# A block kernel's prologue: extra throwaway products in TensorE's pauses, and step 0's state and output put ahead of step 1's transposed blocks

## The chip, the core and the metric

One core of a Trainium2 chip runs the whole program. The metric is device microseconds of one execution; what is compared is the median of several executions.

## The reference, cut to what matters

```python
x = L0_attn_out                                   # (4, 2048, 256)
mod = (silu(c) @ wmod) -> sa, ca, ga, sb, cb, gb  # six rows of 256 for each batch
h = layernorm(x) * (1 + ca) + sa
# attention: rk = h / |h| per head, wk = rk one token earlier, v = h @ Ww.T; chunks of 64 tokens
A = inv(I + tril(wk wk^T * decay, -1))            # per chunk and head, 64 x 64
for chunk in 32 chunks:                           # S: 64 x 64 for each head
    v_new = A @ v - (A @ wk) @ S
    o = (rk * decay) @ S + intra @ v_new
    S = decay**64 * S + (wk * tail).T @ v_new
x = x + ga * (h + (alpha * o) @ Wr.T)
h = layernorm(x) * (1 + cb) + sb
u = silu(h @ w1 * s1) * (h @ w2 * s2)             # 256 -> 1024
u = gelu(u @ h1 * sh1); u = gelu(u @ h2 * sh2)    # 1024 -> 1024, ternary weights
x = x + gb * (u @ w3 * s3)                        # 1024 -> 256
```

## The kernel before, in words

The 2048 tokens are 32 steps of 64. One step takes 64 tokens of all four batches: 256 columns for the dense layers. Each step has an attention part, which hands a state on to the next step, and a dense part (`l1`, `l2`, `l3`, `y`), in which each 128x128 block of ternary weights is multiplied by a rounded high part and a low part of the activations. The attention of a step runs beside the dense part of an earlier one.

Each engine has its own program, and every engine's program is generated from one written list of items: `alone`, then `opening`, then `second`, `third` and `mixed` (steady state, in a hardware loop). An engine skips items that are not its own, and takes its own in the order of the list. So if an item moves in a list, it moves in the queue of every engine that has a part of it. Each engine's queue is in order: an instruction that waits for a semaphore holds everything behind it.

Before the dense layers can start (the first product of `l1`, line 1249) the prologue has to be done. It has these pieces, named as in the lists:

- The modulation rows: `shift(0)` and `shift(1)` (line 1561), and, when the second part of `wmod` has landed, 32 small products with 4 columns (line 1578). VectorE makes columns and gates of them (lines 1150 to 1168), and behind that `unit` of step 0, the normalised rows `r` (line 929).
- `start` turns `h` and `r` on TensorE (lines 1384 and 1388); `gram` multiplies the turned rows with themselves (line 1419); ScalarE copies the result (line 797); GpSimd masks it (line 648).
- `fs`, `expand`, `n` invert the triangular blocks. `n` 3 ends with ScalarE's copy to `diag` (line 751). `solve` 0 is `own` (line 1222) and `inner` (line 1215), `solve` 1 is `corner` (line 1232), and ScalarE copies the new values `vn` (line 756).
- `state` (lines 1534 and 1536, then two copies on VectorE, lines 1059 and 1060), `attn_out` (line 1545, then lines 1070 to 897 on VectorE, and a power on GpSimd, line 636), `norm2` (line 1079), `turn` (line 1554), `ln2` (ScalarE, line 832), `parts` (VectorE, lines 1085 and 1087), and then `l1`.
- For step 1, as far as it is ready: `stats`, `norm`, `square`, `length`, `unit`, `start`, `gram`, `intra`, `fs`, `values`, `pred`. `square` overwrites `r`, so it waits until the last token's row has been copied out by SP (`last_in`, line 531). For step 1 there is a power on GpSimd in `length`.
- `check` on ScalarE (line 766) runs through 11 parts of the raw weights as they land and sums their low bits. `check` 2 is parts 2, 3 and 4; `check` 3 and 4 are one part each; `check` 5 is the last four parts. After the last one `flag` tells whether any bit was set: VectorE reduces, TensorE turns the column, VectorE reduces again, and TensorE reads the flag (`value_load`) and takes one of two programs, the exact one only if a weight isn't representable.
- `warm` (line 1238) multiplies a tile of ones into a bank that nobody reads. `round` casts weights (GpSimd line 659, ScalarE line 771). `residual` is two products on GpSimd (lines 678, 680).

An fp32 product shows as two matmul records in the trace.

Of the kernel before, what the change touches and what calls it, by code (L numbers as in the profile page):

```python
# [15 lines left out]
P = 128  # L16
# [45 lines left out]


CHECKS = {0: (0,), 1: (1,), 2: (2, 3, 4), 3: (5,), 4: (6,), 5: (7, 8, 9, 10)}
WARM_START, WARM_CHAIN, WARM_LINK, WARM_FLAG, WARM_JUMP = 3, 4, 1, 2, 1
ROUNDS_ACT = {2: (4, 5)} | {3 + k: (6 + k,) for k in range(11)}
ROUNDS_POOL = {0: (0, 2), 1: (1, 3)} | {5 + k: (17 + k,) for k in range(5)}

# [44 lines left out]
def main(nc, ctx, sb, sem, sems, x, wts, wv, wr, wmod, cT, scales, s3, decay, const, out):  # L113
# [5 lines left out]
    duo = [ctx.enter_context(nc.psum_tensor(f"duo{i}", [P, 2, 512], F32)) for i in range(2)]  # L119
# [23 lines left out]
    state = sb("state", [NP, 2, DH])  # L143
# [141 lines left out]
    def listed(first, columns, between):  # L285
# [26 lines left out]
    alone = [(*item, 0) if len(item) == 2 else item for item in (  # L312
        ("check", 0), ("ready", 0), ("start", 0), ("spread", 0), ("tables", 0), ("gram", 0), ("heads", 0), ("check", 1), ("values", 0), ("gates", 0), ("warm", WARM_CHAIN),
        ("intra", 0), ("fs", 0), ("fs", 1), ("fs", 2), ("fs", 3), ("expand", 0), ("far", 0), ("stats", 0, 1), ("check", 2), ("n", 1),
        ("warm", WARM_LINK), ("n", 2), ("warm", WARM_LINK), ("n", 3), ("heads", 1), ("warm", WARM_LINK), ("norm", 0, 1), ("round", 0), ("square", 0, 1), ("length", 0, 1),
        ("solve", 0), ("check", 3), ("unit", 0, 1), ("wr", 0), ("keys", 0), ("solve", 1), ("start", 0, 1), ("check", 4), ("round", 1), ("residual", 0), ("state", 0),
        ("gram", 1, 1), ("rg", 0, 1), ("intra", 0, 1), ("check", 5), ("fs", 0, 1), ("attn_out", 0), ("values", 0, 1), ("pred", 0, 1), ("warm_end", WARM_FLAG))]

    opening = [(*item, 0) for item in (
        ("norm2", 0), ("turn", 0), ("fs", 1), ("flag", 0), ("u", 0), ("flag", 1), ("ln2", 0), ("ln2", 1), ("parts", 0), ("residual", 0),
        ("round", 2), ("silu", 0))]
    second = listed([], layers[:2 * HK], {
        ("l1", 0): [("fs", 2, 0)],
        ("l1", 2): [("fs", 3, 0)],
# [58 lines left out]
    def begun(n, items):  # L385

        if items is mixed:
            return min(n + 2, STEPS) if isinstance(n, int) else n + 2
        return 3 if items is third else n + 1
# [87 lines left out]
    with nc.Block() as block:  # L477
# [156 lines left out]
        def _(pool):  # L634
# [17 lines left out]
            def step(n, g, items):  # L652
                def part(name, k, a, phase):
                    now, p = a + 1, phase % 2
                    if name == "round":
                        for u in ROUNDS_POOL.get(k, ()):
                            slot = slice(SLOT * u, SLOT * (u + 1))
                            pool.wait_ge(checked, u // UNIT_SLOTS + 1)
                            pool.tensor_copy(w_hi[:, slot, :], w_raw[:, slot, :]).then_inc(rounded[1], 1)
                    if name == "ready":  # L660
                        pool.wait_ge(near_tables, 1)
                    if name == "stats":
                        stats(a)
                    if name == "length":
                        length(a)
                    if name == "residual":

                        if items is alone:
                            pool.wait_ge(gates_ready, NB)
                        if items is alone:  # L670
                            pool.wait_ge(r_ready, 2)
                        if items is opening:
                            pool.wait_ge(xl_ready, n)
                        pool.wait_ge(h_ready, now)
                        after(pool, x1_ready, a - 2)
                        if items is mixed or items is third and a == n + 2:
                            pool.wait_ge(r_turned, a - 3)
                        pool.tensor_tensor(base[phase % BASES][:], h_of(a)[:], ga, ALU.mult).then_inc(gah_ready, 1)
                        pool.wait_ge(gah_ready, now)
                        pool.tensor_tensor(base[phase % BASES][:], x_of(a)[:], base[phase % BASES][:], ALU.add).then_inc(base_ready, 1)  # L680
                    if name == "rg":
                        if items is alone:
                            pool.wait_ge(heads_ready, 1)
                        pool.wait_ge(rT_ready, now)
                        pool.tensor_tensor(rg[:].rearrange("p (b q) c n -> p b (q c) n", b=NB),
                                           rT[p][:].rearrange("p (b q) c n -> p b (q c) n", b=NB)[:, :, :, 1:C + 1],
                                           head_decay[:].rearrange("p q c n -> p (q c) n").unsqueeze(1).to_broadcast([P, NB, H, C]),
                                           ALU.mult).then_inc(rg_ready, 1)
                    if name == "gram":
                        for e in range(2):  # L690
                            pool.wait_ge(gram_ready[e], now)
                            ins = masked(near, 0, e)
                        ins.then_inc(near_ready, 1)
                        for e in range(2):
                            ins = masked(cross, 1, e)
                        ins.then_inc(cross_ready, 1)
                    if name == "l1":
                        pool.wait_ge(l1_hi, nth(n, k))
                        pool.tensor_tensor(act_lo[0][:, k, :], full[k % 3][:], act_hi[0][:, k, :].bitcast(F32), ALU.subtract).then_inc(l_ready[0], 1)  # L699
                    if name == "far":  # L700

                        if items is alone:
                            pool.wait_ge(inv_ready, now)
                        after(pool, mi_full, a)
                        for e in range(2):
                            ins = masked(far, 2, e)
                        ins.then_inc(far_ready, 1)
                    if (name == "lead" or name == "solve" and k == 0) and items is not alone:
                        pool.wait_ge(inter_full, a)
                        by_head = state[:].rearrange("p (b q) c d -> p b q (c d)", b=NB)  # L710
                        pool.tensor_tensor(by_head, by_head, chunk_decay[:].unsqueeze(1).unsqueeze(3).to_broadcast([P, NB, H // 2, 2 * DH]),
                                           ALU.mult).then_inc(state_decayed, 1)
                    if name == "attn_out":
                        pool.wait_ge(ln2_ve, now)
                        rsqrt(rstd2, ve2, ln2_rstd)

                walk(part, n, g, items)
# [475 lines left out]
        def _(pe):  # L1193
# [40 lines left out]

            def warm(count, bank, cols=512):

                for _ in range(count * 512 // cols):
                    pe.matmul(bank[:, 0:cols], o_state[:, 0, :], o_state[:].rearrange("p q n -> p (q n)")[:, 0:cols], start=True, stop=True)

            def step(general, n, g, items):  # L1240
# [88 lines left out]
                def part(name, k, a, phase):  # L1329
# [25 lines left out]
                                mm = pe.transpose(mlp[b][:, i * P:(i + 1) * P], gate_cols[:, i // KT, i % KT, 2 * b:2 * b + 2, :].rearrange("p b n -> p (b n)"), ident)  # L1355
                            mm.then_inc(gates_spread, 1)
                    if name == "warm":
                        warm(k, duo[0][:, 1, :], P)
                    if name == "warm_end":
                        warm(k, duo[1][:, 1, :])  # L1360
                    if name == "flag" and k == 0:
                        pe.wait_ge(flag_col, 1)
                        pe.transpose(duo[1][0:1, 1, 0:P], any_low[:], ident).then_inc(flag_row, 1)
                        warm(WARM_JUMP, duo[1][:, 0, :])
                    if name == "ready":
                        pe.wait_ge(small_in, 5 * 16)
                    if name == "tables":
# [7 lines left out]
                    if name == "start":  # L1375
# [6 lines left out]
                        for kt in range(KT):  # L1382
                            for b in range(NB):
                                mm = pe.transpose(in_h[:, (b * KT + kt) * P:(b * KT + kt + 1) * P], h_a[:, b, kt * P:(kt + 1) * P], ident)
                        mm.then_inc(hT_full, 1)
                        pe.wait_ge(r_ready, now)
                        for q, (b, hp) in enumerate(pair_of):
                            mm = pe.transpose(in_r[:, q * P:(q + 1) * P], r[:, b, hp * P:(hp + 1) * P], ident)
# [32 lines left out]
                    if name == "pred":  # L1421
# [2 lines left out]
                            pe.wait_ge(ao_scaled, n)  # L1424
                            pe.wait_ge(state_ready, n)
                        if items is not mixed:
                            pe.wait_ge(hT_ready, now if items is alone else begun(n, items))
                            pe.wait_ge(rT_ready, now if items is alone else begun(n, items))
                        if items is alone:
                            pe.wait_ge(state_ready, a)  # L1430
                        for q, c, e in blocks:
                            mm = pe.matmul(duo[0][half(c), e, q * DH:(q + 1) * DH], rT[p][half(e), q, c, 0:C],  # L1432
# [130 lines left out]
                mm.then_inc(mod_full, 1)  # L1563

            pe.wait_ge(warm_set, 1)
            warm(WARM_START, mlp[1][:], P)
            pe.wait_ge(spread_done, 1)
            pe.wait_ge(wmod_in[0], 16)
            shift(0)
            pe.wait_ge(pow_ready, 1)  # L1570
            pe.transpose(solo[1][0:H, 0:P], powers[:], ident).then_inc(pow_turned, 1)
            shift(1)

            pe.wait_ge(spread_done, 2)
            pe.wait_ge(wmod_in[1], 16)
# [3 lines left out]
            mm.then_inc(col_full, 1)  # L1579
            first_step(lambda *args: step(False, *args))  # L1580
            pe.wait_ge(flag_set, 1)
            warm(WARM_JUMP, duo[1][:, 1, :])
            any_bits = pe.value_load(flag_i[0:1, 0:1], min_val=0, max_val=1)
            with pe.If(any_bits < 1):
                program(False)
# [43 lines left out]
```

## Time and profile before

| | us |
|---|---|
| median of 3 runs | 1703.91 |
| lowest, highest | 1701.28, 1704.21 |
| the profiled execution, its own time | 1700.03 |
| its span in the trace | 1698.1 |

| engine | busy us | share of the span |
|---|---|---|
| TensorE (PE) | 1677.2 | 99% |
| VectorE (DVE) | 1144.6 | 67% |
| ScalarE (ACT) | 1004.8 | 59% |
| GpSimd (POOL) | 596.6 | 35% |

Starts are microseconds from the start of the span. The granted clock (PEclk) is TensorE's, as a share of 2.4 GHz; it has two levels, 0.50 (1.2 GHz) and 1.00 (2.4 GHz), and a value between them is a stretch with both. "issue" as the releaser of a wait is time in which nothing that the profile shows was waited for.

### The profile page before, as it was taken

How to read it: one execution, taken by the hardware profiler on the slowest of the kernel's cores; microseconds unless marked ns; L12 is line 12 of the kernel's file. 1: busy time of each engine (PE TensorE's matmuls, PEld its weight loads, DVE VectorE, ACT ScalarE, POOL GpSimd, SP SyncE). 2: the span in 40 equal slices, each digit the busy share in tenths (PEclk: the TensorE clock that was granted, in tenths of full speed). 3: DMA queues.
4: the chain of work that ended last, by engine and by line, in shares of the span. 5: the costliest groups of instructions: out<-in, count | busy, mean ns of one | idle time of the engine just before them, and what ended most of it. 6: DMA issues, size and time to landing. Idle time of an engine off the chain costs nothing.

```text
span 1698.1 us, 59356 instructions
## 1 busy us (share of the span) xinstructions
PE 1677.2 (99%) x24310; PEld 1619.7 (95%) x24310; DVE 1144.6 (67%) x3223; ACT 1004.8 (59%) x2389; POOL 596.6 (35%) x694
## 2 busy tenths in 40 slices
PE   8899999999999999999999999999999999999998
PEld 7798999999999999999999999999999999999998
DVE  5777667776666776766776766776766776766432
ACT  4764665556656556666556665555665555665554
POOL 3544333343333243433243333234333234333101
PEclk8899999999999999999999999999999999999999
DMA  8202223332223332222332222322222332222110
GB/s 279 89 21 41 49 47 61 55 55 43 50 48 56 55 58 42 49 48 56 56 57 44 49 49 53 61 52 44 51 50 49 61 54 44 52 49 42 21 20 8
DMA packets 396492, 92.13 MB, mean 54 GB/s; under 512 B 368372, under 2 KB 388472, under 8 KB 396216
## 3 DMA queue, kind: packets, MB, share of 16 engines
q1 hardware_dynamic: 394224, 85.87, 25.8%
q8 instruction: 197, 3.23, 0.8%
q10 hardware_dynamic: 1992, 2.38, 0.5%
q14 instruction: 79, 0.65, 0.1%
HBM read 45.07 MB, written 30.94 MB: 45 GB/s over the span
## 4 chain that ended last, share of the span: by engine, by line
PE 94%; DVE 2%; POOL 1%; DMA 1%; issue 1%; ACT 1%; SPq 0%; ACTq 0%; DVEq 0%; POOLq 0%
PE mlp L1249 66%; PE mlp L1323 7%; PE solo L1249 3%; PE solo L1407 3%; PE duo L1545 3%; PE solo L1222 2%; PE duo L1215 1%; PE solo L1232 1%; PE duo L1432 1%; PE duo L1210 1%; PE duo L1534 1%; PE duo L1419 1%; PE duo L1536 1%; PE duo L1455 1%; POOL act_lo L699 1%
## 5 line engine op out<-in xcount | busy, mean ns | idle before, releaser
L1249 PE MATMUL mlp<-act_hi,w_hi 128*128 128x256 f32 x4096 | 975.1, 283 | 1.2 <-POOL act_lo L699 0.6
L1249 PE MATMUL mlp<-act_lo,w_hi 128*128 128x256 f32 x4096 | 954.5, 278 | 0.0
L1249 PEld LDWEIGHTS mlp<-act_hi,w_hi 128*128 128x128 f32 x4096 | 771.2, 188 | 12.0 <-POOL act_lo L699 1.4
L1249 PEld LDWEIGHTS mlp<-act_lo,w_hi 128*128 128x128 f32 x4096 | 771.8, 188 | 0.8
L858 ACT ACTIVATE full<-mlp,scale_sb 128x256 f32<-128x256 f32 x512 | 242.6, 474 | 444.1 <-PE mlp L1249 441.8
L961 DVE TENSOR_TENSOR act_lo<-full,act_hi 128x256 fp32r<-128x256 f32 x512 | 260.3, 508 | 276.4 <-ACT act_hi L859 274.2
L699 POOL TENSOR_TENSOR act_lo<-full,act_hi 128x256 fp32r<-128x256 f32 x256 | 186.9, 736 | 484.5 <-ACT act_hi L848 484.5
L859 ACT ACTIVATE act_hi<-mlp,scale_sb 128x256 fp32r<-128x256 f32 x512 | 240.1, 469 | 0.0
L1249 PE MATMUL mlp<-xh,w_hi 128*128 128x256 f32 x768 | 180.5, 278 | 1.3 <-DVE full L1093 1.3
L1249 PE MATMUL mlp<-xl,w_hi 128*128 128x256 f32 x768 | 179.7, 277 | 0.0
L1093 DVE SCALAR_TENSOR_TENSOR full<-mlp,scale_sb,gate 128x256 f32<-128x256 f32 x192 | 92.7, 484 | 87.4 <-ACT gate L843 83.3
L1249 PEld LDWEIGHTS mlp<-xh,w_hi 128*128 128x128 f32 x768 | 144.3, 188 | 3.2 <-DVE full L1093 1.7
L843 ACT ACTIVATE gate<-mlp,scale_sb 128x256 f32<-128x256 f32 x192 | 91.4, 476 | 91.7 <-PE mlp L1249 76.0
L1249 PEld LDWEIGHTS mlp<-xl,w_hi 128*128 128x128 f32 x768 | 144.3, 188 | 0.0
L636 POOL TENSOR_TENSOR rinv<-ssm,minus_half 128x8 f32<-128x8 f32 x32 | 52.8, 1650 | 204.0 <-DVE ssm L926 204.0
L1323 PE MATMUL mlp<-w_hi,act_hi 128*128 128x256 f32 x512 | 122.4, 281 | 0.0
L1323 PE MATMUL mlp<-w_hi,act_lo 128*128 128x256 f32 x512 | 121.8, 279 | 0.0
L848 ACT CAST act_hi<-full 128x256 fp32r<-128x256 f32 x256 | 101.8, 398 | 12.8 <-DVE full L1093 12.8
L648 POOL TENSOR_TENSOR near<-gram,level_mask 128x256 f32<-128x256 f32 x64 | 45.9, 738 | 152.8 <-ACT gram L797 152.8
L1323 PEld LDWEIGHTS mlp<-w_hi,act_hi 128*128 128x128 f32 x512 | 96.1, 188 | 0.1
L1323 PEld LDWEIGHTS mlp<-w_hi,act_lo 128*128 128x128 f32 x512 | 96.1, 188 | 0.0
L636 POOL TENSOR_TENSOR rstd<-ve,minus_half 128x2 f32<-128x2 f32 x64 | 48.2, 754 | 124.4 <-DVE ve L897 121.7
(198 smaller groups left out, 2734.7 us busy)
## 6 DMA issues: line engine op xcount, KB each, us to landing
w_raw<-in_wts SPq DMA_DIRECT2D x22, 512.0 KB, 5.2
kg<-r SPq DMA_DIRECT2D x64, 126.0 KB
xin<-in_x SPq DMA_DIRECT2D x62, 128.0 KB, 2.8
out_y<-y SPq DMA_DIRECT2D x62, 128.0 KB, 2.5
x_squares<-o_state SPq DMA_DIRECT2D x30, 256.0 KB, 3.2
vn<-x_squares SPq DMA_DIRECT2D x120, 64.0 KB, 2.2
h_squares<-near SPq DMA_DIRECT2D x28, 256.0 KB, 3.3
hT<-h_squares SPq DMA_DIRECT2D x112, 64.0 KB, 2.2
```

The lines of the kernel that those rows point to most:

```text
L636: pool.tensor_tensor(dst[:], src[:], minus_half[:, 0:src.shape[1]], ALU.pow).then_inc(done, 1)
L699: pool.tensor_tensor(act_lo[0][:, k, :], full[k % 3][:], act_hi[0][:, k, :].bitcast(F32), ALU.subtract).then_inc(l_ready[0], 1)
L843: act.activation(gate[k % 2][:], gated[k % 3][:, 0:TOK], ACT.Silu, scale=scale_sb[:, 0, k:k + 1]).then_inc(l_act[0], 1)
L848: act.copy(act_hi[0][:, j, :], full[j % 3][:]).then_inc(l1_hi, 1)
L858: act.activation(full[k % 2][:], mlp[k % 2][:, 0:TOK], ACT.Gelu, scale=s)
L859: act.activation(act_hi[layer % 2][:, k, :], mlp[k % 2][:, 0:TOK], ACT.Gelu, scale=s).then_inc(l_act[layer], 1)
L961: dve.tensor_tensor(act_lo[layer % 2][:, k, :], full[k % 2][:], act_hi[layer % 2][:, k, :].bitcast(F32), ALU.subtract).then_inc(l_ready[la ...
L1093: dve.scalar_tensor_tensor(full[k % 3][:], up, s, gate[k % 2][:], ALU.mult, ALU.mult).then_inc(prod_ready, 1)
L1249: mm = pe.matmul(dst, *general_ops, start=is_first and i == 0, stop=is_last and i == 1)
L1323: mm = pe.matmul(mlp[k][:, 0:D], *ops, start=j == 0 and i == 0, stop=j == HK - 1 and i == 1)
L1407: mm = pe.matmul(solo[0][:, b * D:(b + 1) * D], hT[:, b, kt, :], wv_sb[:, kt, :], start=kt == 0, stop=kt == KT - 1)
L1545: mm = pe.matmul(duo[1][:, 0, b * D:(b + 1) * D], o_state[:, b * (H // 2) + hp, :], wr_turned[:, hp, :], start=hp == 0, stop=hp == H // 2 - 1)
```

## The change

Only the prologue's lists and throwaway products change; the lists `second`, `third` and `mixed` are as they were.

1. Throwaway products. `WARM_START` and the three `WARM_LINK` and `WARM_CHAIN` products have 512 columns each and no longer 128 (four times fewer products for as many columns); `WARM_CHAIN` is 5 and no longer 4. New: 2 products of 512 behind `shift(1)`, 3 between the two halves of step 0's `start`, 2 ahead of step 1's `gram`. Near the flag, products are cut to 128 columns: 12 of them (1536 columns, before 1024) in `warm_end`, 8 (1024 columns, before 512) in `flag`, 4 (512 columns, as before) ahead of the `value_load`.
2. `residual` 0, `keys` 0 and `wr` 0 come ahead of step 1's `square`. On GpSimd `residual` 0 now waits for the second `h` instead of the second `r`. `round` 1 comes ahead of `solve`.
3. `state` 0 comes ahead of step 1's `unit`, and `attn_out` 0 ahead of step 1's `start`.
4. `values`, `pred`, `intra` and `fs` 0 of step 1, and `warm_end`, go from `alone` to `opening`, behind `norm2` and `turn`.

```diff
-WARM_START, WARM_CHAIN, WARM_LINK, WARM_FLAG, WARM_JUMP = 3, 4, 1, 2, 1
+WARM_START, WARM_SHIFT, WARM_TURN, WARM_CHAIN, WARM_LINK, WARM_GRAM, WARM_FLAG, WARM_JUMP = 3, 2, 3, 5, 1, 2, 3, 1
+PIECE_FLAG, PIECE_JUMP = 128, 128
...
-        ("warm", WARM_LINK), ("n", 2), ("warm", WARM_LINK), ("n", 3), ("heads", 1), ("warm", WARM_LINK), ("norm", 0, 1), ("round", 0), ("square", 0, 1), ("length", 0, 1),
-        ("solve", 0), ("check", 3), ("unit", 0, 1), ("wr", 0), ("keys", 0), ("solve", 1), ("start", 0, 1), ("check", 4), ("round", 1), ("residual", 0), ("state", 0),
-        ("gram", 1, 1), ("rg", 0, 1), ("intra", 0, 1), ("check", 5), ("fs", 0, 1), ("attn_out", 0), ("values", 0, 1), ("pred", 0, 1), ("warm_end", WARM_FLAG))]
+        ("warm", WARM_LINK), ("n", 2), ("warm", WARM_LINK), ("n", 3), ("heads", 1), ("warm", WARM_LINK), ("norm", 0, 1), ("round", 0), ("residual", 0),
+        ("keys", 0), ("wr", 0), ("square", 0, 1), ("length", 0, 1), ("round", 1), ("solve", 0), ("solve", 1), ("check", 3), ("state", 0), ("unit", 0, 1),
+        ("attn_out", 0), ("start", 0, 1), ("check", 4), ("warm_wait", WARM_GRAM), ("gram", 1, 1), ("rg", 0, 1), ("check", 5))]
...
-        ("norm2", 0), ("turn", 0), ("fs", 1), ("flag", 0), ("u", 0), ("flag", 1), ("ln2", 0), ("ln2", 1), ("parts", 0), ("residual", 0),
-        ("round", 2), ("silu", 0))]
+        ("norm2", 0), ("turn", 0), ("values", 0), ("pred", 0), ("warm_end", WARM_FLAG), ("intra", 0), ("fs", 0), ("fs", 1), ("flag", 0), ("u", 0), ("flag", 1), ("ln2", 0), ("ln2", 1),
+        ("parts", 0), ("residual", 0), ("round", 2), ("silu", 0))]
...
                         if items is alone:
-                            pool.wait_ge(r_ready, 2)
+                            pool.wait_ge(h_ready, 2)
...
-                for _ in range(count * 512 // cols):
+                for _ in range(count * (512 // cols)):
...
                     if name == "warm":
-                        warm(k, duo[0][:, 1, :], P)
+                        warm(k, duo[0][:, 1, :])
+                    if name == "warm_wait":
+                        warm(k, solo[1][:])
                     if name == "warm_end":
-                        warm(k, duo[1][:, 1, :])
+                        warm(k, duo[1][:, 1, :], PIECE_FLAG)
...
                         pe.transpose(duo[1][0:1, 1, 0:P], any_low[:], ident).then_inc(flag_row, 1)
-                        warm(WARM_JUMP, duo[1][:, 0, :])
+                        warm(2 * WARM_JUMP, duo[1][:, 0, :], PIECE_JUMP)
...
                         mm.then_inc(hT_full, 1)
+                        if items is alone and a == 0:
+                            warm(WARM_TURN, mlp[1][:])
                         pe.wait_ge(r_ready, now)
...
-                            pe.wait_ge(hT_ready, now if items is alone else begun(n, items))
-                            pe.wait_ge(rT_ready, now if items is alone else begun(n, items))
-                        if items is alone:
+                            pe.wait_ge(hT_ready, begun(n, items))
+                            pe.wait_ge(rT_ready, begun(n, items))
+                        if items is opening:
                             pe.wait_ge(state_ready, a)
...
-            warm(WARM_START, mlp[1][:], P)
+            warm(WARM_START, mlp[1][:])
...
             shift(1)
+            warm(WARM_SHIFT, mlp[1][:])
...
-            warm(WARM_JUMP, duo[1][:, 1, :])
+            warm(WARM_JUMP, duo[1][:, 1, :], PIECE_JUMP)
```

## Rows read from the trace of the kernel before

**Rows 1.** Windows: stretch, its length, busy us (instructions) per engine, granted clock, DMA share, GB/s

```profile
12.60:18.80 6.20, 6.20 (x30) 5.83 (x29) 3.87 (x16) 1.86 (x2) 1.94 (x2) 0.50 0.62 202
26.20:39.80 13.60, 11.95 (x232) 10.85 (x232) 10.37 (x50) 8.31 (x11) 4.50 (x6) 1.00 0.94 332
39.80:50.10 10.30, 8.97 (x164) 8.32 (x163) 7.80 (x9) 5.93 (x8) 7.14 (x5) 0.51 0.93 316
60.30:63.80 3.50, 3.46 (x5) 1.11 (x5) 2.09 (x5) 3.50 (x10) 0.00 (x0) 0.52 0.03 7
200.00:1000.00 800.00, 799.96 (x11827) 778.12 (x11826) 561.38 (x1586) 477.19 (x1163) 282.00 (x324) 1.00 0.28 52
```

**Rows 2.** Timeline of TensorE's products: start, us, line, tiles, shape, records, idle before

```profile
11.73 6.15 PE L1578 MATMUL mlp<-scT,wmod_sb 128*128 128x4 f32 x32 [1.80 <-DMA wmod_sb<-in_wmod]
...
27.85 3.74 PE L1238 MATMUL duo<-o_state 128*128 128x128 f32 x32
31.64 1.12 PE L1199 MATMUL duo<-inv,cross 64*64 64x32 f32 x32
...
44.29 1.92 PE L1232 MATMUL solo<-vn,mi 32*32 32x64 f32 x32 [0.52 <-issue]
...
48.36 1.13 PE L1534 MATMUL duo<-intra,vn 64*64 64x64 f32 x32 [0.25 <-issue]
49.24 1.08 PE L1536 MATMUL duo<-vn,kg 64*64 64x64 f32 x32
50.23 0.70 PE L1419 MATMUL mlp<-rT 64*64 64x65 f32 x32
...
60.49 3.54 PE L1238 MATMUL duo<-o_state 128*128 128x512 f32 x4
64.00 0.35 PE L1249 MATMUL mlp<-xh,w_hi 128*128 128x256 f32 x1
```

**Rows 3.** Chain that ended last, 36 to 52: start, us, what

```profile
38.46 1.90 issue
```

**Rows 4.** Timeline of VectorE, lines of square, unit, wr, keys, attn_out and parts

```profile
40.47 0.69 DVE L922 TENSOR_TENSOR r<-x 128x512 f32<-128x512 f32 x1 [1.55 <-DMA last<-r]
...
43.84 1.50 DVE L929 TENSOR_TENSOR r<-x,rinv 128x512 f32<-128x512 f32 x1 [1.75 <-POOL rinv L636]
45.26 2.40 DVE L978 TENSOR_SCALAR wr_turned<-wr_turned,gam 128x256 f32<-128x256 f32 x2
47.58 0.68 DVE L998 TENSOR_TENSOR kg<-kg,tail_decay 128x512 f32<-128x512 f32 x1
...
54.20 0.68 DVE L1070 TENSOR_TENSOR x<-duo,mods 128x512 f32<-128x512 f32 x1
...
57.09 0.17 DVE L897 TENSOR_SCALAR ve<-mv 128x2 f32<-128x2 f32 x1
...
63.16 0.69 DVE L1087 TENSOR_TENSOR xl<-h,xh 128x512 fp32r<-128x512 f32 x1
```

**Rows 5.** Timeline of ScalarE, parts 4 and last of check, diag, vn, gram

```profile
33.07 1.91 ACT L766 ACTIVATE low_bits<-w_raw 128x2048 f32<-128x2048 uint16 x1 [0.33 <-DMA w_raw<-in_wts]
...
37.08 0.84 ACT L751 ACTIVATE diag<-duo,con 128x256 f32<-128x256 f32 x2 [2.00 <-PE duo L1466]
...
46.24 0.59 ACT L756 COPY vn<-solo 128x512 f32<-128x512 f32 x1 [0.16 <-PE solo L1232]
...
50.98 0.65 ACT L797 COPY gram<-mlp 128x256 f32<-128x256 f32 x2 [1.21 <-PE mlp L1419]
...
57.81 1.91 ACT L766 ACTIVATE low_bits<-w_raw 128x2048 f32<-128x2048 uint16 x1
```

**Rows 6.** DMA queues, 38 to 39: packets, MB, share of 16 engines' time

```profile
q8 instruction: 1, 0.02, 6.0%
```

**Rows 7.** Timeline of GpSimd, step 1's power in length

```profile
42.17 1.64 POOL L636 TENSOR_TENSOR rinv<-ssm,minus_half 128x8 f32<-128x8 f32 x1 [6.26 <-DVE ssm L926]
```

**Rows 8.** Timeline of weight loads, the first one of l1 behind the flag

```profile
63.97 0.19 PEld L1249 LDWEIGHTS mlp<-xh,w_hi 128*128 128x128 f32 x1 [1.43 <-issue]
```

## The prediction

> **What bounds the kernel now.** I read the page first: TensorE is busy for 99% of the span. Then the windows: from 200 to 1000 us it is busy for 799.96 of 800 us at granted clock 1.00 [rows 1]. No list of that stretch is edited, so it stays as long as it is. What can move is the moment at which the dense layers start, the first product of l1 at 64.00 [rows 2]; whatever it moves by, the end moves by: what follows is built on it in every engine, and in the long stretch TensorE has no idle time that could take a shift up. So the case is a prologue of 64.0 us, of which the edits can reach some part.
>
> In the prologue the windows show the clock at 0.50 in three stretches: 12.60 to 18.80, 39.80 to 50.10, and 60.30 to 63.80 [rows 1]. TensorE had paused before each: 1.80 us for wmod [rows 2], 1.90 us in own [rows 3], and before the flag. At 0.50 a run of 32 small products takes 1.92 us and at 1.00 it takes 1.12; a record with 128 columns takes 3.74 / 32 = 0.117 us at 1.00 and 3.54 / 16 = 0.221 at 0.50 (the four 512-column records count as 16) [rows 2].
>
> Then I asked what l1 waits for, going backwards through the timelines. It starts at 64.00; xl is written at 63.16 + 0.69 = 63.85 [rows 4]; ahead of that stand ln2 and the last check on ScalarE, which starts at 57.81, and ScalarE goes from its copy of gram at 50.98 through the four checks of check 5 without a pause [rows 5]. Call the start of that copy G. Last check = G + 6.83, xl = G + 12.87, l1 = G + 13.02. The edited lists keep check 5 whole and behind gram, and ln2 behind it. So **two numbers decide: G, and how long after G l1 starts**, where the products behind the flag now count: they begin at 60.49 = G + 9.51 and end when l1 starts [rows 2].
>
> **The change part by part: what comes before G.**
>
> (a) The two products behind shift(1) (512 columns, two records each: 16 x 0.117 = 1.9 us) fill the 1.80 us pause [rows 2] and cost nothing. If the clock stays, the 32 records of line 1578 take about half of their 6.15 us and end near 14.8 and not at 17.88. Behind it gates, unit, start, gram and fs are earlier, by at most 3.1 us and at the least by none (the 3 products in start add 24 x 0.117 = 2.8 us at full clock, 5.3 at half, and lie in the wait for r). From about 1.3 upwards it no longer matters which: ScalarE can't copy to diag before part 4 of check is done. That check waited for its DMA, starts at 33.07, and with 1.91 and some 0.2 for reading its sum (an estimate by the smallest row, 0.17 [rows 4]) ends near 35.2 [rows 5]; the loads are not edited, and the DMA share is 0.94 [rows 1]. So diag starts at 35.2 instead of 37.08: -1.9. I take this end, since the expected lead is 1.3 to 2.6. The other end is 38.4 (+1.3, rival 3).
>
> (b) From diag to vn: before from 37.08 + 0.84 = 37.92 to 46.24 + 0.59 = 46.83 [rows 5], 8.9 us. In it is a pause of 1.90 us in the middle of own, in which nothing awaited is seen, and after which the clock is 0.51 [rows 1, 3]. New at full clock: own 1.12, inner 1.12, a copy 0.35 (half of the gram copy's 0.65), corner 1.12, vn 0.59, and five hand-overs of 0.05: 4.55, to 36.0 + 4.55 = 40.6. With the pause 42.5. With everything at half clock and the pause: 3 x 1.92 + 0.35 + 0.59 + 0.25 + 1.9 = 8.85, to 44.9.
> Which? The queue that brings instructions has one packet just as TensorE stands still [rows 6]; the pause looks like a missing block of instructions. The edits take some 50 records and their weight loads out of the queue ahead, so that the block's end falls into inner and no longer into own; behind it the consumption is as fast and the DMA engines are as loaded. I keep the pause, and take 42.5.
> The Trainium skill, "Runtime: NRT & Kernel Launch", section Instruction fetch mechanics, says that crossing a block boundary is mostly hidden, since fetching runs ahead of dispatch. The 1.90 us above say otherwise for this stretch. By the rule vn would be there at 40.6, the no-pause end (rival 1).
>
> (c) The VectorE queue before state. In the 1.55 us wait for the DMA of the last row [rows 4] now stand keys (0.68) and wr (2.40, slow beside GpSimd; it will have residual beside it again). norm ends at 40.47 - 1.55 = 38.92 before and 1.9 earlier now, 37.0; 37.0 + 0.68 + 2.40 = 40.1, still ahead of 40.47. So square stays at 40.47, which the DMA sets (it is issued behind loads that don't move), and 3.1 us of later VectorE work are gone. With (a) at nothing, square is late by 1.5. GpSimd's residual moves to the same place and its power is free by 42.0; round 1 sits behind the power and slows unit, as before.
> The Trainium skill, "GPSIMD Engine Reference", section Specifications, says that GpSimd shares VectorE's path to SBUF and contends with instructions that have two SBUF inputs or run in a two-port mode. It speaks against putting keys and wr beside residual; the trace agrees for wr (2.40 for two) and for unit (1.50), not for keys, 0.68 beside residual.
>
> (d) state to G. square, its sum and its floor end at 40.47 + 0.69 + 0.69 + 0.17 = 42.0 [rows 4], the power at 42.1 + 1.64 = 43.75 [rows 7]. state's products took 48.36 to 50.32 at half clock; at full 1.96 x 1.12 / 1.92 = 1.2 [rows 2]: 42.5 + 1.2 = 43.7. VectorE's two copies of 0.69: 45.1. unit 0.68 to 1.50, I take 1.1: 46.2. attn_out, whose products run beside unit, 54.20 to 57.26 = 3.06 on VectorE [rows 4]: 49.2. The rT copies 0.9 (0.69 and 0.17, one gap): 50.1. gram 0.70 [rows 2]: 50.8. **G = 50.9 against 50.98: nothing.** What it costs: step 1's gram, which ScalarE needs before the last four checks, now stands behind attn_out on VectorE; what it gains is that xn is there at 50 instead of 59, but nobody can use it, as ln2 stands behind the checks. The bounds: without the pause VectorE is the limit: 42.0 + 1.38, unit from 43.75 to 44.85, + 3.06 + 0.9 + 0.7 gives G = 49.6 (-1.4). With the pause and the clock fallen behind it (corner 1.92, state 1.96, gram 1.2): 52.9 (+1.9).
>
> **What comes after G.** values and pred are TensorE's before 54, and warm_end (24 records, 2.8 us) ends near 56, though the flag comes at G + 9.2 = 60.1: over 3 us of pause, so I expect half clock at the flag, as before. There are now 16 + 8 = 24 records of 128 columns for 16 before: at half clock as long as the 3.3 us that it took to rise [rows 1], 15 records, then 9 x 0.117 = 1.05: 4.4 us, l1 = G + 13.9. Bounds: at full clock 2.8 us, and xl (G + 12.9) is later; all at half 5.3 us, and up to 1.43 us for reading the flag and the jump, seen as a gap before the first load of l1 [rows 8] but hidden there under the last long product; short pieces hide less: G + 16.2. I take G + 13.9.
>
> **Sum.** l1 at 50.9 + 13.9 = 64.8, +0.8 us. The profiled execution would take 1700.03 + 0.8 = 1700.8; it stands 3.9 below the median of the runs shown, 1703.91, so the median becomes **1704.7**.
>
> **Rivals.**
> Rival 1, the pause goes and the clock holds: G = 49.6, and l1 at xl, G + 12.9 = 62.5: -1.5, 1702.4. For it: three filled pauses; against it: the pause in own was not a wait for data. If the last row's DMA lands 2 us earlier as well (its wait was 1.55 [rows 4]), it is -3.5, 1700.4.
> Rival 2, slower: the pause stays and the clock falls behind it as it did before, since state, attn_out and gram now all stand in one line on it. G = 52.9, l1 = G + 14.9 (one more us for the jump): 67.8, +3.8, 1707.7. It decides if TensorE stands still for 1.9 us in inner. For it: the same pause was followed by 0.51 before. Against it: more columns stand just ahead.
> Rival 3, the clock falls during line 1578 after all, whose products have 4 columns. Then the 3 products in start hold the turn of r: 5.3 us and not 2.8. r is turned 1.3 late, diag 38.4 less what the earlier rise gives back; with the tail of the forecast +2.2, 1706.1.
>
> **How the numbers follow.** What a measurement of this kernel can tell from no change is about 0.2%, 3.4 us: under 1700.5 or over 1707.3. Forecast (a shift within 1 us of +0.8) 0.45, rival 1 0.27 (0.12 of it with the early DMA or luck of the runs, below 1700.5), rival 2 0.18, rival 3 0.10. Same: 0.45 + 0.15 + 0.10 = 0.70; faster 0.12; slower 0.18. The runs shown span 2.9 us by themselves, which is in the range: 1701.0 to 1708.0 leaves most of the early-DMA case and a part of rival 2 out.
>
> **What would show it.** Clock 1.00 through 12 to 18 and line 1578 near 3.1 us (a); diag's copy at 35.2 behind part 4 of check (a); a pause of 1 to 2 us in inner or corner (b); square still at about 40.5, released by the DMA (c); ScalarE idle twice between vn and gram and G near 50.9 (d); 0.50 at the flag and l1 at 64 to 65.5 (tail). I am wrong if l1 starts before 62 or after 67, or if the stretch behind it changes its length.

## The result, and the profile after

The changed kernel takes 1708.02 us (median of 11 executions, 1703.56 to 1712.88) against 1703.97 for the kernel before (11, 1701.28 to 1705.17): ratio 1.0026, 95% interval 1.0014 to 1.0039. That is +4.05 us, slower, and the interval leaves out 1. (The ratios here and below are those on record; they are not the quotients of the two medians, and differ from them by up to 0.1%.) I had forecast no change, 1704.7, range 1701.0 to 1708.0. The profiled execution is the fastest of the eleven, 1703.56 us, span 1701.6. Its lines are one higher or more than those of before (l1 is line 1250).

Windows of the changed kernel (columns as in [rows 1]):

```profile
12.60:18.80 6.20, 6.20 (x42) 5.00 (x43) 4.80 (x19) 1.28 (x1) 1.79 (x2) 1.00 0.53 193
26.20:39.80 13.60, 11.69 (x239) 6.77 (x237) 11.46 (x42) 8.13 (x12) 6.54 (x7) 1.00 0.89 308
41.50:48.30 6.80, 5.49 (x72) 4.58 (x73) 4.34 (x6) 2.14 (x3) 4.08 (x3) 0.50 0.97 352
62.00:65.40 3.40, 3.40 (x17) 3.40 (x18) 1.78 (x5) 3.40 (x11) 0.00 (x0) 0.50 0.03 7
200.00:1000.00 800.00, 799.80 (x11828) 778.09 (x11827) 560.02 (x1583) 478.45 (x1166) 284.11 (x327) 1.00 0.28 52
```

The clock is at 1.00 where it was 0.50 before (12.6 to 18.8), and at 0.50 from 41.5 to 48.3 and at the flag. The long stretch is as full as before. Timelines of TensorE, ScalarE and VectorE (columns as in [rows 2, 4, 5]):

```profile
12.56 3.71 PE L1584 MATMUL mlp<-scT,wmod_sb 128*128 128x4 f32 x32
...
37.46 1.15 PE L1223 MATMUL solo<-v,diag 64*64 64x64 f32 x32 [1.17 <-issue]
38.41 1.10 PE L1216 MATMUL duo<-diag,far 64*64 64x32 f32 x32
40.03 1.08 PE L1233 MATMUL solo<-vn,mi 32*32 32x64 f32 x32 [0.52 <-issue]
41.88 1.13 PE L1539 MATMUL duo<-intra,vn 64*64 64x64 f32 x32 [0.77 <-ACT vn L757]
...
44.79 3.70 PE L1550 MATMUL duo<-wr_turned,o_state 128*128 128x256 f32 x8 [0.93 <-DVE o_state L1060]
...
62.14 4.40 PE L1239 MATMUL duo<-o_state 128*128 128x128 f32 x24
66.29 0.37 PE L1250 MATMUL mlp<-xh,w_hi 128*128 128x256 f32 x1
```
```profile
34.52 1.91 ACT L767 ACTIVATE low_bits<-w_raw 128x2048 f32<-128x2048 uint16 x1 [1.82 <-DMA w_raw<-in_wts]
...
36.43 0.82 ACT L752 ACTIVATE diag<-duo,con 128x256 f32<-128x256 f32 x2
...
52.89 0.65 ACT L798 COPY gram<-mlp 128x256 f32<-128x256 f32 x2 [1.43 <-PE mlp L1424]
```
```profile
37.65 2.70 DVE L979 TENSOR_SCALAR wr_turned<-wr_turned,gam 128x256 f32<-128x256 f32 x2
...
41.89 0.69 DVE L923 TENSOR_TENSOR r<-x 128x512 f32<-128x512 f32 x1 [1.54 <-DMA last<-r]
...
45.26 1.50 DVE L930 TENSOR_TENSOR r<-x,rinv 128x512 f32<-128x512 f32 x1
48.60 0.69 DVE L1071 TENSOR_TENSOR x<-duo,mods 128x512 f32<-128x512 f32 x1 [1.84 <-PE duo L1550]
```

Line 1578's 32 records (now 1584) took 3.71 us for 6.15 and diag started 0.65 earlier. But G is 52.89 (50.98 in [rows 5]) and l1 starts at 66.29 (64.00 in [rows 2]): +2.3 us. By when the same activation of ScalarE starts in each of the two traces, the changed kernel is +2.1 to +2.8 us late from 83 us to 1340 us, and +3.4 from 1480 us to the end; a little over 1 us is lost in the unrolled steps behind the loop. The new loss to see is in the last row: VectorE stands idle for 1.84 us, waiting for attn_out's products, which took 3.70 us at half clock.

### The profile page after: what moved, and what is told of

It is laid out like the page before. It is cut to its first block, busy times and chain, and to the rows that moved or that the text cites. A ratio compares the mean times of both kernels' runs of the same rounds, so it can differ in the third digit from the quotient of the medians.

```text
span 1701.6 us, 59346 instructions
## 1 busy us (share of the span) xinstructions
PE 1679.1 (99%) x24306; PEld 1615.0 (95%) x24306; DVE 1143.5 (67%) x3223; ACT 1005.2 (59%) x2389; POOL 596.4 (35%) x694
## 4 chain that ended last, share of the span: by engine, by line
PE 94%; DVE 2%; ACT 1%; DMA 1%; POOL 1%; issue 1%; SPq 0%; ACTq 0%; DVEq 0%
PE mlp L1250 65%; PE mlp L1324 7%; PE duo L1550 3%; PE solo L1250 3%; PE solo L1412 3%; PE solo L1223 2%; PE duo L1216 1%; PE duo L1437 1%; PE solo L1233 1%; PE duo L1211 1%; PE duo L1539 1%; PE duo L1541 1%; PE duo L1424 1%; PE duo L1460 1%; POOL act_lo L700 1%
## 5 line engine op out<-in xcount | busy, mean ns | idle before, releaser
L637 POOL TENSOR_TENSOR rstd<-ve,minus_half 128x2 f32<-128x2 f32 x64 | 48.3, 754 | 125.9 <-DVE ve L898 123.0
```

Source lines behind the costliest of these rows:

```text
L637: pool.tensor_tensor(dst[:], src[:], minus_half[:, 0:src.shape[1]], ALU.pow).then_inc(done, 1)
```

## The experiments

They ran on four chips. Each ratio is against runs of the kernel before beside it on the same chip, whose medians were 1698.17 to 1700.53. "Gap" means: TensorE stands still inside a run of products of one kind, and the profile names no releaser.

**e1 to e4: the change in three parts**, and two of them together.

```diff
 e1_front: before, and
+WARM_SHIFT 2, WARM_TURN 3, WARM_CHAIN 5; START, CHAIN and LINK with 512 columns
 e2_lists: before, and the two lists of after without warm_wait, its waits
 e3_tail: before, and
+warm_end 12 x 128, flag 8 x 128, ahead of value_load 4 x 128
 e4_front_lists: after, and
-the three edits of e3
```

> The kernel before with the front's throwaway products alone: 2 products of 512 columns behind shift(1), 3 in step 0's start, WARM_CHAIN 5, and all those up to n 3 with 512 columns; lists and flag products as before. Theory (the loss comes from the lists, which put step 1's gram and with it ScalarE's last four checks behind attn_out): the front gains, gram's copy on ScalarE starts 0.5 to 1.5 us before 50.98, and the time is 0 to 1.5 us under before. Rival (the loss comes from clock and throwaway products, wherever they stand): 2 us or more over before, with more time at half clock.

> The kernel before with the changed lists and waits alone; no product of the front or of the flag is changed, none ahead of step 1's gram. Theory lists: gram's copy at 52 to 54, l1 at 65 to 67, the time 2 to 4 us over before. Rival (front or flag products make the loss): within 1 us of before.

> The kernel before with the flag's products alone in their new form: 12 of 128 columns in warm_end, 8 of 128 columns behind the flag's column, 4 of 128 ahead of reading the flag. Theory tail small: 24 records of 128 columns for 16, at half clock 1.0 us more behind the flag, l1 at 64.9 to 65.3, the time +0.5 to +1.5 us. Rival (short pieces leave reading the flag and the jump uncovered, or the clock rises a window later and l1's own products run at half clock): +2 to +5 us.

> The changed kernel with the flag's products as before (2 of 512 in warm_end, 1 behind the column, 1 ahead of reading the flag): front and lists without the tail. Theory lists: gram's copy near 52.9 as in the changed kernel, l1 at 65.9, the time +2 to +3.5 us over before, some 0.5 under the changed kernel. Rival tail: the time is back within 1 us of before and its runs agree with each other as those of before do.

| run | median us | ratio, 95% interval | l1 in its trace |
|---|---|---|---|
| e1_front | 1709.59 | 1.0053, 1.0041 to 1.0065 | 64.81 |
| e2_lists | 1704.90 | 1.0027, 1.0018 to 1.0036 | 69.08 |
| e3_tail | 1707.08 | 1.0040, 1.0027 to 1.0053 | 65.20 |
| e4_front_lists | 1709.54 | 1.0064, 1.0051 to 1.0077 | 68.25 |

Both theories missed. The front and the tail each cost more by themselves than the whole change (1.0026), the lists as much, and the front, with l1 at nearly the old time, costs most of the three. In e1 the delay against the trace of before grows from 0.4 us at 242 to 9.4 at 1362, where both programs do the same work. The waits of TensorE in e1 from 200 to 1400 us follow (engine, line, releaser: us in total, times, longest); before has none of them:

```profile
PE duo L1199 <- issue: 4.4, 6, 1.1
PE duo L1215 <- issue: 3.7, 7, 0.9
```

e1 has 24 throwaway products fewer in TensorE's queue than before, e4 22 fewer, e3 20 more; e2 has as many, and the whole change 2 fewer. From 200 to 1690 us waits like these add up to 4.7 us in e3 and 3.8 in e4, and to 0.3 in e2. Hence the next question: is it the number of instructions ahead of the loop?

**e5 to e8: the count, and the checks.**

```diff
 e5_front_count: e1, and
-START and CHAIN with 512 columns
+START and CHAIN with 128 columns (40 products, as before)
 e6_fewer: before, and
-START, CHAIN, LINK: 40 products of 128 columns
+START, CHAIN, LINK: 10 products of 512 columns
 e7_after_count: after, and
-warm(WARM_SHIFT, mlp[1][:])
+warm(WARM_SHIFT, mlp[1][:], 256)
 e8_checks: before, and
-2: (2, 3, 4), 3: (5,), 4: (6,), 5: (7, 8, 9, 10)
+2: (2, 3, 4), 6: (5,), 3: (6,), 4: (7,), 5: (8, 9, 10)
+("check", 6) ahead of ("solve", 0)
```

> The front's products as in the first experiment, the same columns at the same places, but cut so that TensorE's queue has exactly as many products as in the kernel before (WARM_START and WARM_CHAIN in pieces of 128 columns, the others 512: 40 products as before, where the first experiment had 16). Theory placement (the number of instructions ahead of the steady loop decides where the blocks end in which TensorE's instructions are brought, and a block's end in a run of small products costs a pause): no pause without a reason from 200 to 1400 us, the time within 2 us of before, some 7 us under the first experiment. Rival (the columns themselves or the clock make the loss): again 6 us or more over before, with pauses of 8 us in the loop.

> The kernel before with its own throwaway products up to n 3 cut larger: the same columns at the same places in 10 products of 512 and not in 40 of 128, nothing else. Theory placement: the prologue is unchanged, but pauses without a seen reason appear in the steady loop, and the time is +3 to +9 us. Rival: within 1 us of before.

> The changed kernel with the 2 products behind shift(1) cut into 4 of 256 columns: as many products in TensorE's queue as before. Theory placement: its loop is free of such pauses in all runs and its runs agree as those of before do (within 4 us); what is left over before is the prologue, +1.5 to +4 us. Rival: 6 us or more over before, or runs that span 9 us again.

> The kernel before, ScalarE's queue alone changed: part 5 of the checks ahead of solve, 6 and 7 in the two later places, so that three and not four checks stand behind step 1's gram. Theory (ScalarE's four checks behind gram decide when l1 starts): gram's copy near 51, last check near 55.7 and not 57.8, l1 1.5 to 2.1 us earlier, near 62.2, the time 1.5 to 2 us under before. Rival (the flag's products and the clock decide, or the parts have not landed): less than 0.5 us under before.

| run | median us | ratio, 95% interval |
|---|---|---|
| e5_front_count | 1697.43 | 0.9996, 0.9988 to 1.0005 |
| e6_fewer | 1710.13 | 1.0065, 1.0050 to 1.0079 |
| e7_after_count | 1700.69 | 1.0021, 1.0009 to 1.0033 |
| e8_checks | 1697.48 | 0.9995, 0.9986 to 1.0004 |

e6 has the columns, lists, waits and work of before, l1 at 63.97, and is 12 us slower. It spends 7.8 of them here (waits of TensorE, 200 to 1400 us):

```profile
PE duo L1215 <- issue: 4.1, 9, 0.8
PE duo L1199 <- issue: 3.7, 8, 0.9
```

e5, which has e1's columns and before's count, has none of it. So **the number of products ahead of the loop decides**, as the theory of placement said. For the changed kernel it decides little: e7, 2 products longer, keeps a loss (its interval overlaps that of the whole change) and its scatter (1697.54 to 1712.91), which its rival had forecast. In its trace, the slowest of its runs, G is 60.70. e8 moved the last check from 57.81 to 56.99 though G was at 52.25, but l1 came at 64.84: ScalarE now waits 1.58 us for the turned xn, so the checks and the xn chain were nearly tied before, and no gain clear of the scatter is left.

**e9 and e12: the changed kernel again; e10 and e11: two orders.**

```diff
 e9_after_again, e12_after_look: after, unchanged
 e10_front_checks: e5 and e8 together
 e11_after_order: e7, and
-("attn_out", 0), ("start", 0, 1), ("check", 4), ("warm_wait", WARM_GRAM), ("gram", 1, 1), ("rg", 0, 1),
+("start", 0, 1), ("check", 4), ("warm_wait", WARM_GRAM), ("gram", 1, 1), ("rg", 0, 1), ("attn_out", 0),
```

> The changed kernel itself, on the chip of the other experiments, for a second trace beside its first one (which was its fastest run). Theory placement: its queue is 2 products (8 instructions) shorter than before, so most of its loss is in the prologue (pauses in inner, half clock behind them, gram's copy at 53 to 58), and up to 3 us in pauses in the loop; +3 to +6 us over before. Rival: the loop alone loses 6 us or more, as in the sixth experiment.

> The changed kernel once more, one look, for a third trace of it: where two traces of one kernel differ, theory placement expects a pause of 1 to 3 us at a block's end in the prologue in one and not in the other, and a stretch of half clock behind it. Rival: they differ evenly over the loop.

> The fifth and the eighth experiment together: the lists of before, the front's products at an unchanged count, and ScalarE's checks one place earlier. If both gains are real and add up (each was 0.7 us, inside its interval): 1 to 3 us under before, l1 at 62 to 63.5. Rival (the flag's products and the turn of xn, not the checks, set l1 by now): no more than 0.7 us under before.

> The seventh experiment (changed kernel at the count of before) with step 0's attn_out put behind step 1's start and gram again, and nothing else. Theory order (gram behind attn_out on VectorE and TensorE delays ScalarE's last four checks): gram's copy 3 us earlier than in the changed kernel, near 49 to 51, the time 2 to 4 us under the seventh experiment and at or under before. Rival (the pauses and the clock make the loss, in whatever order): within 1 us of the seventh experiment.

e9: 1704.20, ratio 1.0030 (1.0020 to 1.0040); e12, one execution: 1700.95. Their timelines differ at two places, e9 first:

```profile
34.73 1.05 PE L1204 MATMUL duo<-step_and_inv,step_nt 32*32 32x64 f32 x58
38.37 0.31 PE L1204 MATMUL duo<-step_and_inv,step_nt 32*32 32x64 f32 x6 [2.59 <-issue]
...
43.86 0.72 PE L1216 MATMUL duo<-diag,far 64*64 64x32 f32 x20
45.68 0.54 PE L1216 MATMUL duo<-diag,far 64*64 64x32 f32 x12 [1.09 <-issue]
...
48.59 0.76 PE L1539 MATMUL duo<-intra,vn 64*64 64x64 f32 x32 [0.77 <-ACT vn L757]
...
51.12 3.75 PE L1550 MATMUL duo<-wr_turned,o_state 128*128 128x256 f32 x8 [0.91 <-DVE o_state L1060]
```
```profile
38.71 0.75 PE L1216 MATMUL duo<-diag,far 64*64 64x32 f32 x20
41.37 0.54 PE L1216 MATMUL duo<-diag,far 64*64 64x32 f32 x12 [1.91 <-issue]
...
44.72 1.14 PE L1539 MATMUL duo<-intra,vn 64*64 64x64 f32 x32 [0.77 <-ACT vn L757]
...
47.62 3.75 PE L1550 MATMUL duo<-wr_turned,o_state 128*128 128x256 f32 x8 [0.92 <-DVE o_state L1060]
```

The gap stands in inner, where the prediction had put it, behind its 20th record both times, and in e4 too. The third trace, the profiled one above, has none. e9 has a second gap, 2.59 us in n 2. e7, 2 products (4 records) longer, has both gaps 4 records earlier:

```profile
35.31 0.98 PE L1204 MATMUL duo<-step_and_inv,step_nt 32*32 32x64 f32 x54
38.92 0.46 PE L1204 MATMUL duo<-step_and_inv,step_nt 32*32 32x64 f32 x10 [2.63 <-issue]
...
44.52 0.64 PE L1216 MATMUL duo<-diag,far 64*64 64x32 f32 x16
46.63 0.66 PE L1216 MATMUL duo<-diag,far 64*64 64x32 f32 x16 [1.48 <-issue]
```

In order of profiled execution, e12, e9: G is 52.89, 55.76 and 59.26, and l1 66.29, 68.77 and 72.42. From 200 to 1690 us none of the three has more than 0.6 us of such waits, so the loss of the changed kernel is for the most part in its prologue. What lies behind l1 isn't constant either: it took 1635.3, 1630.3 and 1632.9 us, and 1634.1 in the trace of before. That is why e12, with l1 4.8 us later than in that trace, still took only 1700.95 us.

e10: 1699.05, ratio 0.9998 (0.9989 to 1.0007); the rival holds, the two small gains don't add up, and ScalarE waits 1.58 us for xn again. e11: 1705.96, ratio 1.0039 (1.0025 to 1.0053), against 1.0021 for e7: the order theory's forecast of a shorter time failed. G in its trace was 54.91 and so earlier than the 60.70 of e7's, but xn is turned only at 61.88 and ScalarE's copy of v, ahead of ln2 in its queue, waits for the products of values, which now stand behind that turn at half clock; ln2 starts at 66.90, and l1 comes 17.79 us behind G.

**e13 to e16: the gap and the clock.**

```diff
 e13_delay_loads: before, and SP's loads of the weights
+if i == 5: sp.wait_ge(own_ready, 1)
 e14_plus12: before, and
-WARM_START: 12 products of 128 columns
+WARM_START: 15 products of 96 columns
 e15_fill: e7, and
+4 products of 128 columns ahead of corner, of state's and of attn_out's products
-WARM_FLAG 3
+WARM_FLAG 0
 e16_after_count_look: e7, unchanged
```

> The kernel before, but SP issues the weights from part 5 on only when own is done (own_ready), so that little DMA traffic lies beside own. The prologue gets longer behind it; read the pause alone. Theory instruction blocks behind a loaded DMA: the pause in own, 1.3 to 1.9 us in the traces so far with the block's end there, shrinks to under 0.6 us. Rival (the pause belongs to the place or to another cause and not to the traffic): it stays at 1.3 to 1.9 us.

> The kernel before with WARM_START cut into 15 products of 96 columns for 12 of 128: 3 products more, 12 instructions, ahead of everything. Theory placement: the block's end moves from own's 5th record ahead of own, into the wait for diag, where TensorE stands idle anyway; no pause within own. In the steady loop it shows how near the next bad place is: within 1 us of before if 12 more are harmless as 8 fewer were, or up to +5 us. Rival: the pause in own stays where it is.

> The seventh experiment (changed kernel at the count of before) with four 128-column products in each of three waits behind own (ahead of corner, of state, and of attn_out, the last on an identity matrix), and none in warm_end instead of 12, so that the count is unchanged. Theory clock (behind the first pause the clock falls, and attn_out's products at half clock hold VectorE up): attn_out's products take 2.0 us and not 3.75, gram's copy comes 1.5 to 2 us earlier and the time is 1 to 2 us under the seventh experiment, 1700.7 against 1698.2 of before there. Rival (the pauses themselves make the loss): no difference over 0.5 us.

> The seventh experiment once more, one look, beside the others of this call. Expected: a loop without pauses; if 2.6 us stand in n 2 again, gram's copy is near 59 to 61, if not near 53 to 56.

e13 is one execution, 1707.08 us, longer as expected. Around own the DMA share is 0.00 over four us, and 0.86 in before (36.5 to 40.5). The window of e13, then own's products:

```profile
34.00:38.00 4.00, 3.83 (x119) 3.36 (x119) 3.35 (x11) 2.42 (x4) 0.41 (x1) 1.00 0.00 1
```
```profile
36.62 1.29 PE L1224 MATMUL solo<-v,diag 64*64 64x64 f32 x31
```

31 of own's 32 records now run through in 1.29 us where there were 4 and a gap of 1.90 [rows 3]. The same gap had been there in the traces of e2 and e3 (1.63 each), e8 (1.35) and e10 (1.37), so the forecast came true. But it shows less than it seems to: e5 has as many products ahead of own as e10, a DMA share of 0.93 just before own and 1.01 in its first us, and no gap either.

```profile
39.53 1.30 PE L1222 MATMUL solo<-v,diag 64*64 64x64 f32 x31
```

So in one of six traces with the traffic the gap at this place was missing too, and one trace without the traffic can't show that the traffic makes it.

e14: 1700.65, ratio 1.0003 (0.9994 to 1.0012). Its timeline:

```profile
36.66 1.05 PE L1238 MATMUL duo<-o_state 128*128 128x128 f32 x7
39.05 0.27 PE L1238 MATMUL duo<-o_state 128*128 128x128 f32 x1 [1.35 <-issue]
39.29 1.15 PE L1222 MATMUL solo<-v,diag 64*64 64x64 f32 x32
```

Three products (6 records) more, and the gap is 5 records earlier, in the last throwaway products; own is whole. It still holds own up, since diag is done at 37.63. The loop stays nearly clean at +3 products.

e16 (one execution, 1699.09) is e7 again, and this time without a gap and at full clock; its TensorE and ScalarE:

```profile
37.89 1.15 PE L1223 MATMUL solo<-v,diag 64*64 64x64 f32 x32 [0.18 <-issue]
38.84 1.10 PE L1216 MATMUL duo<-diag,far 64*64 64x32 f32 x32
...
42.31 0.69 PE L1539 MATMUL duo<-intra,vn 64*64 64x64 f32 x32 [0.77 <-ACT vn L757]
...
44.40 1.97 PE L1550 MATMUL duo<-wr_turned,o_state 128*128 128x256 f32 x8 [0.92 <-DVE o_state L1060]
...
64.22 0.43 PE L1250 MATMUL mlp<-xh,w_hi 128*128 128x256 f32 x1
```
```profile
50.87 0.65 ACT L798 COPY gram<-mlp 128x256 f32<-128x256 f32 x2 [1.54 <-PE mlp L1424]
```

e15: 1701.86, ratio 1.0013 (1.0001 to 1.0025), runs from 1698.17 to 1708.41. In its trace the clock holds to 58.3, attn_out's products take 1.96 us and G is 50.77, as the clock theory said; its l1, behind a flag whose wait is no longer filled, is at 65.00. But e16, with nothing filled, held its clock as well. The ratio of e15 is lower than e7's 1.0021, but the intervals overlap, and the scatter stays: whether filling the waits gains anything is not shown.

**e17 and e18: the lists with the gap elsewhere, and a best version.**

```diff
 e17_lists_plus12: e2, and WARM_START as in e14
 e18_best: e10, and WARM_START as in e14
```

> The second experiment (the kernel before with the changed lists and waits alone, 1.0027 of before) with WARM_START as 15 products of 96 columns for 12 of 128, as in the fourteenth, and nothing else. Theory (the lists are slower because a block's end in own or inner now delays the one line state, attn_out, gram, checks): with the block's end ahead of own the loss falls from +4.5 us to +1.5 or less, gram's copy at 50.5 to 53. Rival (the new order itself costs, wherever the pause is): +3 to +5 us again, gram's copy at 54 or later.

> The kernel before with the front's products at its count, ScalarE's checks one place earlier, and the 3 more products that put the block's end ahead of own: no pause within own, l1 at 62 to 64. If the pause in own costs what stands behind it: 1 to 2.5 us under before. Rival (l1 is set by the turn and ln2 behind the flag, and the rest is scatter): within 1 us of before.

e17: 1704.02, ratio 1.0021 (1.0012 to 1.0030). own is whole, and still, timeline of TensorE and of ScalarE:

```profile
37.39 0.27 PE L1238 MATMUL duo<-o_state 128*128 128x128 f32 x1 [0.79 <-issue]
37.63 1.15 PE L1222 MATMUL solo<-v,diag 64*64 64x64 f32 x32
...
44.95 3.75 PE L1545 MATMUL duo<-wr_turned,o_state 128*128 128x256 f32 x8 [0.92 <-DVE o_state L1059]
```
```profile
53.54 0.65 ACT L797 COPY gram<-mlp 128x256 f32<-128x256 f32 x2 [1.72 <-PE mlp L1419]
```

+3.5 us where e2 had +4.5, intervals overlapping: the time is the rival's (+3 to +5), though G is a little under its 54. Without a gap in own the lists still lose, and attn_out's products are at half clock again (VectorE waits 2.31 us for them). e18: 1700.55, ratio 0.9999 (0.9990 to 1.0008). No version beats the kernel before.

## Why the prediction was wrong

The forecast's own path exists, but as one of several that the same program takes, and one step of it was priced at the wrong clock. Rival 2 (0.18) came out on the median nearly to the microsecond, 1707.7 written and 1708.02 measured. That is luck in part: it had half clock behind a gap of 1.9 us in inner, but no half clock for attn_out, and the profiled execution has its G of 52.9 without any gap.

The forecast's steps beside those of five traces, in us:

| | start of diag | from there to state's first product | from there to G | G | from G to l1 |
|---|---|---|---|---|---|
| forecast | 35.2 | 7.3 | 8.4 | 50.9 | 13.9 |
| profiled execution | 36.43 | 5.45 | 11.01 | 52.89 | 13.40 |
| e12 | 36.71 | 8.01 | 11.04 | 55.76 | 13.01 |
| e9 | 41.57 | 7.02 | 10.67 | 59.26 | 13.16 |
| e15 | 36.13 | 6.20 | 8.44 | 50.77 | 14.23 |
| e16 | 36.84 | 5.47 | 8.56 | 50.87 | 13.35 |

- **What bounds it.** Right in the main: a prologue that shifts the rest. G and l1 moved together in every trace of the changed kernel.
- **(a)** Right in direction: the clock held, but line 1584 took 3.71 us and not 3.1. With those columns ahead (twelve traces) the 32 records took 3.63 to 5.08 us, without them (eight traces) 3.99 to 6.90. diag started at 36.43 and not 35.2, since the weights' part 4 landed 1.45 us later in this execution; in e9 it was 41.57, behind a gap in n 2 that the prediction had not thought of.
- **(b)** The place of the gap was right, inner. That its place follows from the number of instructions ahead of it is now shown: 3 products more move it by 5 records (e14, e17), 2 products more by 4 (e7 against e9), and the two gaps of one trace are 126 records apart in e7 as in e9. Why it opens is not shown. In e13 it was gone where the DMA engines stood idle, but it was missing at shares of 0.93 and more too, in own in e5 and in inner in the profiled execution and in e16. Its size in inner was none, 1.91 and 1.09 us in the three traces of the changed kernel. The Trainium skill, "Runtime: NRT & Kernel Launch", section Instruction fetch mechanics, has instructions arrive in blocks, fetched ahead, and calls a boundary mostly hidden; the profiled execution, e5 and e16 agree, and e9 and e12 don't.
- **(c)** Right in mechanism: square waited 1.54 us for its DMA behind keys and wr (2.70), though at 41.89 and not at 40.47. In the profiled execution it held nothing up.
- **(d), the step that failed:** "attn_out, whose products run beside unit". It took the 1.96 us of TensorE at full clock for granted. At half clock they are 3.70 to 3.75, in all three traces of the changed kernel and in e2, e4, e7 and e17, and VectorE waits for them, by 1.84 us in the profiled execution. From state's first product to G the forecast had 8.4 us; at full clock it was 8.44 and 8.56 (e15, e16), and in the three traces 10.67 to 11.04. I had priced half clock only in the rival, and there only for corner, state and gram. In the old order attn_out's products ran at half clock for a part too (2.23 to 3.52 us in the nine traces of experiments with the old lists, 1.96 in before), but there they stand behind gram and can't delay G.
- **Luck in G.** e15 and e16 have the G of the forecast, but by two errors that cancel: diag 0.9 and 1.6 us late, and no gap where 1.9 us were kept.
- **The tail** was mis-sized a little: 13.0 to 13.4 us behind G and not 13.9.
- **"It stays as long as it is"**, said of the long stretch: nearly so for this change, but not for the reason given, that none of its lists is edited. Front alone has 24 products fewer, the tail alone 20 more, and with the two ahead of gram the whole has 2 fewer. By themselves they cost 0.53% and 0.40%, much of it in the loop.

Open: why the gaps come in one execution and not in the next. Half clock in the products of step 0's start precedes each of the three 2.6 us gaps of n 2 (e7, e9, e11), but e12 has it too, without such a gap. Open too is why the clock falls: the profiled execution and e16 have the same three waits of 0.5 to 0.9 us between own and attn_out, and it fell only in the first, where TensorE had also stood 1.17 us ahead of own (0.18 in e16). A count that puts both of the prologue's block ends at harmless places was not tried.

## What to carry to other kernels

A throwaway product is also an instruction: before crediting it with a clock, count how it moves everything behind it in its engine's queue, and compare variants at an equal count. When a reorder puts products on the path that had stood behind it, price them at both clocks: here that was 1.97 us against 3.75. And where the runs of a kernel scatter more after a change (9.3 us for 3.9), take a second trace before explaining the first.

## What the runs showed that I had not expected

- Replacing 40 throwaway products of 128 columns by 10 of 512, with nothing else changed, cost 12 us in 1700 (e6), most of it as gaps in runs of small products (17 in the two groups shown, 7.8 us together, none longer than 0.9), although the DMA engines are busy only 0.28 of that time.
- Where a gap opened in the prologue, at DMA shares above 0.85, it took 0.3 us (e1) to 2.7 us (e11). The same program has it in one execution and not in the next (e7 and e16; e9, e12 and the profiled execution).
- A few products more or fewer did no harm to the loop (-2 and +3 left it nearly clean), 20 or more did: +20, -22, -24 and -30.
